# A new order within a tile of the scan, the carry in a spare column of h, a fifth product of w and B on GpSimd, and e minus g summed on TensorE

## The reference

```python
u, z = split(in_proj(seq)); u = silu(conv(u))
dt, Bm, Cm = split(x_proj(u))
dt = softplus(dt_proj(dt) + bias)
def step(h, ...):                        # h: 128 channels x 16 states
    h = exp(dt_t * A) * h + (dt_t * u_t) * B_t
    y = sum over states of h * C_t
y = (ys + u * D) * silu(z);  x = x + out_proj(y)
```

## Time and profile before

| | us |
|---|---|
| median of 3 runs | 1975.07 (1973.82 to 1977.28) |
| the profiled execution | 1973.6 |
| its span | 1971.8 |
| busy: PE, PE weight loads | 1445.4, 980.9 |
| busy: DVE, ACT, POOL | 1359.6, 928.1, 1138.6 |

### The profile page before, as it was taken

How to read it: one execution, slowest core, us unless ns; L and a number is a source line. 1 busy time by engine, 2 the same in 40 slices (tenths; PEclk the granted TensorE clock), 3 DMA queues, 4 the chain that set the end, 5 groups by cost and what they waited for, 6 DMA issues and landing times. The chain is left out here.

```text
span 1971.8 us, 28551 instructions
## 1 busy us (share of the span) xinstructions
PE 1445.4 (73%) x7776; PEld 980.9 (50%) x7777; DVE 1359.6 (69%) x1913; ACT 928.1 (47%) x1695; POOL 1138.6 (58%) x788
## 2 busy tenths in 40 slices
PE   6666766667656599999956766666667662799993
PEld 4333333333314499999834333333333222799992
DVE  2899999999995422222143999999999967444443
ACT  6666677667743011111136666677666731011111
POOL 0687788888880244444302888888878850355540
PEclk9889898998968699999968788998998866899996
DMA  3655566555638110111034565566555634111114
GB/s 110 147 135 121 129 144 146 125 126 134 145 79 354 54 41 32 38 37 36 26 126 98 129 138 121 129 143 139 134 121 135 148 136 188 38 48 48 47 41 152
DMA packets 75964, 217.61 MB, mean 110 GB/s; under 512 B 11856, under 2 KB 27408, under 8 KB 72592
## 3 DMA queue, kind: packets, MB, share of 16 engines
q1 hardware_dynamic: 67664, 194.53, 38.9%
q0 software_dynamic: 8256, 22.56, 3.5%
HBM read 178.34 MB, written 38.70 MB: 110 GB/s over the span
## 5 line engine op out<-in xcount | busy, mean ns | idle before, releaser
L669 POOL TENSOR_TENSOR L_hc<-L_h,L_cbq 128x1536 f32<-128x1536 f32 x192 | 660.1, 3438 | 210.6 <-DVE L_h L587 207.5
L492 ACT ACTIVATE ps<-L_dwq,L_negA 128x384 f32<-128x384 f32 x768 | 426.7, 574 | 227.4 <-DVE L_h L587 215.5
L364 PE MATMUL ps<-L_hc,same 128*32 128x384 f32 x1536 | 190.0, 571 | 238.9 <-POOL L_hc L669 238.9
L574 DVE TENSOR_TENSOR L_dbu<-L_dwq,ps 128x768 f32<-128x768 f32 x288 | 270.7, 941 | 29.4 <-DVE L_carry L649 13.1
L587 DVE TENSOR_TENSOR_SCAN L_h<-ps,L_h,L_dbu 128x384 f32<-128x384 f32 x288 | 275.0, 1002 | 12.9 <-ACT ps L492 12.8
L587 DVE TENSOR_TENSOR_SCAN L_h<-ps,L_carry,L_dbu 128x384 f32<-128x384 f32 x288 | 274.2, 1001 | 6.5 <-DVE L_dbu L574 4.7
L364 PEld LDWEIGHTS ps<-L_hc,same 128*32 128x32 f32 x1536 | 31.5, 113 | 358.2 <-POOL L_hc L669 324.3
L1151 DVE COPY Xn<-L_w 128x2048 f32 x86 | 107.6, 1253 | 117.1 <-PE ps L1101 108.3
L1134 ACT ACTIVATE L0e_hT<-ps 128x512 f32<-128x512 f32 x86 | 51.3, 597 | 267.2 <-PE ps L1101 267.2
L678 POOL TENSOR_TENSOR L_dbp<-L_dwq,L_cbq 128x768 f32<-128x768 f32 x96 | 175.1, 1824 | 0.0
L323 PE MATMUL ps<-Xn,L_fold 128*128 (+1 forms) x480 | 103.3, 368 | 89.2 <-DVE L_dw L595 89.2
(11 more groups left out here) (278 smaller groups left out, 2301.4 us busy)
## 6 DMA issues: line engine op xcount, KB each, us to landing
L_dwq<-dw_rows SPq DMA_DIRECT2D x192, 384.0 KB, 6.2
L_cbq<-cb_rows SPq DMA_DIRECT2D x192, 240.0 KB, 9.9
dw_rows<-L_dw SPq DMA_DIRECT2D x48, 384.0 KB, 2.3
L_w<-in_up SPq DMA_DIRECT2D x16, 1024.0 KB, 11.7
L_w<-in_down SPq DMA_DIRECT2D x8, 1024.0 KB, 26.6
tok_rows<-Xn SPq DMA_DIRECT2D x6, 768.0 KB, 13.1
L0s_got<-results SPq DMA_DIRECT2D x18, 256.0 KB, 2.9
L1s_got<-results SPq DMA_DIRECT2D x18, 256.0 KB, 3.5
```

The source lines that it names most:

```text
L364: mm = nc.tensor.matmul(y_ps[g * QW:(g + 1) * QW, :], same[:, 0:QW], hc[:, (k % 2) * Q + g, :], start=False, stop=(k == Q - 1))
L492: nc.scalar.activation(da(r, c), dwq[:, r, c % Q, 0, :], ACT.Exp, scale=negA[:, 0, c:c + 1]).then_inc(sem["da"], 1)
L574: nc.vector.tensor_tensor(dbu[:, at:at + 2, :], dwq[:, r, 2 * i:2 * i + 2, 1, :], spread(b_ps(r, k)), ALU.mult).then_inc(sem["dbu"], 1)
L669: nc.gpsimd.tensor_tensor(hc[:, at:at + Q, :], h[:, Q * k:Q * k + Q, :], cbq[:, r, k, :].unsqueeze(1).to_broadcast([P, Q, T]), ALU.mult).t ...
```

## The change

Five edits, all in the state-space block:

1. DVE's products of a tile go from six to five (`dbu` gets ten slots, no ring); POOL makes columns 10 and 11 too, in a new product at the head of its tile, from a sixth row of spread B (`QR` from 5 to 6).
2. `h` gets a spare column element (T + 1) that keeps the state from which each image starts; a scan reads its start from `h` itself, and the copy to `carry` and the wait for it go.
3. `lost` goes from POOL; TensorE adds e and, by a matrix of -1 on the diagonal (`minus`), subtracts g: four matmuls where three stood.
4. DVE: `times_u` stands after the tile's first scan (before: after the fourth), `gate` after the fourth (before: after the sixth). ACT: the block with the table loads stands after column 6 (before 7).
5. PE: within a tile, `spread_b` for k = 2 goes first, `u_in` is cut in two around the sum of y of the tile before, `z_in` follows, and the projections of tile t+2 come ahead of `sum_y(t, r, 0)`.

The core of the diff:

```diff
-QR = Q + 1
+QR = Q + 2
+SILU_AT = 6
...
-        carry = sb("carry", [P, 2, N])
+        carry = sb("carry", [P, N])
-        dbu = sb("dbu", [P, 6, T])
-        dbp = sb("dbp", [P, Q, T])
-        h = sb("h", [P, N, T])
+        dbu = sb("dbu", [P, 10, T])
+        dbp = sb("dbp", [P, 6, T])
+        h = sb("h", [P, N, T + 1])
...
             def add_log(t):
                 pe.wait_ge(sem["l"], t + 1)
                 nc.tensor.matmul(ua_ps, ident[:], sp["l"][:], start=False, stop=False)
-                pe.wait_ge(sem["lost"], t + 1)
-                nc.tensor.matmul(ua_ps, ident[:], sp["a"][:], start=False, stop=True).then_inc(sem["dt"], 1)
+                pe.wait_ge(sem["g"], t + 1)
+                nc.tensor.matmul(ua_ps, ident[:], sp["e"][:], start=False, stop=False)
+                nc.tensor.matmul(ua_ps, minus[:], sp["g"][:], start=False, stop=True).then_inc(sem["dt"], 1)
...
+                spread_b(t, r, 2)
+                if more == 2:
+                    u_in(t + 2, img2, (0, 1))
+                if not first:
+                    sum_y(t - 1, 1 - r, Q - 1)
+                if more == 2:
+                    u_in(t + 2, img2, (2, 3, 4))
                 if more:
-                    add_relu(t + 1)
-                    add_log(t + 1)
                     pe.wait_ge(sem["bc_out"], t + 2)
                     wait(pe, sem["res"], t - 1)
                     z_in(t + 1, img1)
-                if not first:
-                    sum_y(t - 1, 1 - r, Q - 1)
-                if more == 2:
-                    u_in(t + 2, img2, range(5))
-                spread_b(t, r, 2)
                 skip(t, r)
-                sum_y(t, r, 0)
-                if more:
-                    spread_b(t + 1, 1 - r, 0)
                 if more == 2:
                     project_dt(t + 2, r)
                     pe.wait_ge(sem["zs"], t + 2)
                     project_bc(t + 2, r)
+                sum_y(t, r, 0)
+                if more:
+                    spread_b(t + 1, 1 - r, 0)
...
                 sum_y(t, r, 2)
+                if more == 2:
+                    add_relu(t + 2)
+                    add_log(t + 2)
...
-                    if c == 7 and more:
+                    if c == SILU_AT and more:
...
                     k, i = (j + 1) // 2, (j + 1) % 2
-                    if k < Q - 1:
+                    if 2 * k + i < 5:
                         times_b(t, r, p, k, i)
                     elif j == N // 2 - 1 and not last:
                         times_b(t + 1, 1 - r, p + r, 0, 0)
                     scan(t, 2 * j, slot)
+                    if j == 0 and not last:
+                        times_u(t + 1, 1 - r, [(s_dw_row[r], 16 * (p + 1))])
                     scan(t, 2 * j + 1, slot)
-                    if j == 1 and not last:
-                        times_u(t + 1, 1 - r, [(s_dw_row[r], 16 * (p + 1))])
                     if not (isinstance(t, int) and t == 0):
-                        if j == 2:
+                        if j == 1:
                             gate(t - 1, 1 - r)
...
-                if not last:
-                    dve.wait_ge(sem["scan"], (2 * p + 2) * N)
-                    nc.vector.tensor_copy(carry[:, 1, :], h[:, :, T - 1]).then_inc(sem["carry"], 1)
-                    dve.wait_ge(sem["carry"], p + 2)
...
             def tile(t, r, p, last):
+                times_b(t, r, p, 0)
                 for k in range(Q):
                     times_c(t, r, p, k)
                     if k < 2:
-                        times_b(t, r, p, k)
-                    if k == 2 and not last:
-                        lost(t + 2)
+                        times_b(t, r, p, k + 1)
```

More of the change, by code:

```diff
@@ L258, in mamba @@
         sem = {k: new(f"{L}_{k}") for k in
-               ("u_in z_in u zs bc dt_in bc_out abs relu e f g l lost dt dt_out w b dbu dbu_p da scan carry hc skip y yz out "
+               ("u_in z_in u zs bc dt_in bc_out abs relu e f g l dt dt_out w b dbu dbu_p da scan carry hc skip y yz out "
                 "res").split()}
@@ L567, in times_b @@
                     dve.wait_ge(s_dw[r], 64 * (p + 1))
[L568 to L573, removed]
+                at = 4 * k + 2 * i
+                wait(dve, sem["scan"], (t - 1) * N + at + 2)
                 nc.vector.tensor_tensor(dbu[:, at:at + 2, :], dwq[:, r, 2 * i:2 * i + 2, 1, :], spread(b_ps(r, k)),
@@ L577, in scan @@
             def scan(t, c, slot):
-                k, g = c // Q, c % Q
+                k = c // Q
                 dve.wait_ge(sem["da"], t * N + c + 1)
-                if k < Q - 1:
-                    dve.wait_ge(sem["dbu"], 6 * t + c // 2 + 1)
+                if c < 10:
+                    dve.wait_ge(sem["dbu"], 5 * t + c // 2 + 1)
                 else:
-                    dve.wait_ge(sem["dbu_p"], 2 * t + g // 2 + 1)
+                    dve.wait_ge(sem["dbu_p"], 3 * t + (c - 10) // 2 + 1)
                 wait(dve, sem["hc"], Q * (t - 1) + k + 1)
[L585 to L588, removed]
+                first = h[:, c, T - 1:T] if slot is None else h[:, c, T - slot:T - slot + 1] if isinstance(slot, int) \
+                    else h[:, c, bass.ds(T - slot, 1)]
+                nc.vector.tensor_tensor_scan(h[:, c, 0:T], da(t % 2 if isinstance(t, int) else int(slot is None), c),
+                                             dbu[:, c, :] if c < 10 else dbp[:, c - 10, :], first, ALU.mult, ALU.add
                                              ).then_inc(sem["scan"], 1)
@@ L612, in _ @@
             nc.vector.tensor_scalar(diagD[:], ident[:], par("D"), None, ALU.mult).then_inc(s_fold, 1)
+            nc.vector.tensor_scalar(minus[:], ident[:], -1.0, None, ALU.mult).then_inc(s_fold, 1)
             times_u(0, 0, ())
             dve.wait_ge(s_tok, 6)
-            nc.vector.tensor_tensor(carry[:, 1, :].rearrange("p (k g) -> p k g", k=Q),
+            nc.vector.tensor_tensor(carry[:].rearrange("p (k g) -> p k g", k=Q),
                                     m["ones"][:, 0:N].rearrange("p (k g) -> p k g", k=Q),
@@ L676, in times_b @@
                     pool.wait_ge(s_dw[r], 64 * (p + 1))
-                    wait(pool, sem["scan"], t * N)
-                nc.gpsimd.tensor_tensor(dbp[:, 2 * i:2 * i + 2, :], dwq[:, r, 2 * i:2 * i + 2, 1, :],
-                                        spread(cbq[:, r, Q, :]), ALU.mult).then_inc(sem["dbu_p"], 1)
-            lost(0)
-            lost(1)
+                wait(pool, sem["scan"], (t - 1) * N + 12 + 2 * i)
+                groups, row = (2, Q + 1) if i == 0 else (2 * i - 2, Q)
+                nc.gpsimd.tensor_tensor(dbp[:, 2 * i:2 * i + 2, :], dwq[:, r, groups:groups + 2, 1, :],
+                                        spread(cbq[:, r, row, :]), ALU.mult).then_inc(sem["dbu_p"], 1)
             q = {k: tok[:, 2 + i:3 + i] for i, k in enumerate("arefgl")}
@@ L1370, in pack @@
     state = g("x_proj_w")[4:].reshape(2, Q, Q, P)
-    put("bc", np.concatenate([state[1].transpose(1, 0, 2), state[0, Q - 1][:, None]], 1).reshape(Q * QR, P).T)
+    put("bc", np.concatenate([state[1].transpose(1, 0, 2), state[0, Q - 1][:, None], state[0, Q - 2][:, None]], 1).reshape(Q * QR, P).T)
     put("brep", np.repeat(state[0].reshape(N, P), QW, 0).T)
```

19 lines of the change are left out of this document (9 added, 10 removed).

## The result

The changed kernel takes 2046.21 us (median of 4 runs, 2043.46 to 2047.22), against 1976.14 us for the kernel before in the same series: a ratio of 1.0354 (95% interval 1.0336 to 1.0372). It is slower by 3.5%.

The account below looks back on a forecast made before the run. DVE set the old 22.37 us period; a wait cycle through four engines, 23.49 us plus 0.5 for the clock, would set 24.0. 44 intervals gave +72 us, less 3, plus 1.5 for the median: 2044 us, range 2008 to 2092.

Parts of the forecast that it names:

- DVE's list: DVE's own work per tile, forecast to fall from 21.41 to 20.56 us, below the old period of 22.37 us.
- the ring: Wait cycle hc2, softplus sum, take_dt, times_u, scans, back to hc2: forecast to set the period, 24.0 us (23.5 to 24.6); 82%.
- the clock's share: Extra time per tile from TensorE's lowered clock between hc2's end and take_dt: 0.5 us, bounds 0 and 0.84 + 0.3.
- hc2's end to take_dt, full clock: From the end of POOL's third hc product to ACT's take_dt: 3.13 us plus 0.64 for one more matmul, 3.77.
- take_dt to times_u: From the start of ACT's take_dt to the start of DVE's times_u, which it releases: 0.79 us.
- times_u to the end of scan 7 (with ACT's hold): DVE's new order from times_u through scan 7, 10.00 us, plus 0.3 us waiting for ACT's table-load block.
- end of scan 7 to hc2's end: POOL's two hc products and one dbp product after DVE's scan 7: 8.63 us.
- no element is left out: Reason given for excluding any gain in POOL's hc products from 385-element rows; cost taken as 0, at most 0.15 us each.
- -3 us for the ends of the layers: After each layer's last times_u DVE's shorter work counts, one or two products less in each layer: -3 us.
- Rival A: DVE's work sets the time: period 20.9 us, 1907 us in total, faster; chance 9%.
- Rival B: No change in time: the round trip is 22.4 us, 1.1 us shorter than any sum at full clock; chance 3%.
- Rival C: TensorE's clock falls on every softplus sum: round trip 26.8 us, +192 us, 2167 us in total; chance 6%.

Follow-up runs that it names:

- adds_first: The changed kernel with TensorE's softplus sum for tile t+2 moved ahead of the third sum of y; 1896.09 us, ratio 0.9616 to the kernel before.
- old_places: The changed kernel with times_u, the gate and ACT's table block back at their old places in the tile; 2033.42 us, ratio 1.0317 to the kernel before.
- The fillers: The changed kernel with ten unused TensorE matmuls ahead of the second sum of y and five ahead of the third; 1995.02 us, ratio 1.0115.
- before_u_early: The kernel before with times_u alone moved behind the tile's first scan; 2063.3 us, ratio 1.0461.

## Why the prediction was right

**The mechanism.** It forecast that the softplus sum behind the third sum of y, with times_u moved ahead of scan 1, closes a ring through four engines that is longer than DVE's list. The wait ahead of times_u is there in every tile, adds_first removes it and with it 150 us, and the product on DVE is free with the ring and costs 37 us without. That DVE's saving is wasted behind the ring is shown, too. Of the runs that change something on this ring, all but old_places moved the way that it says, and in old_places another ring closed.

**The size, 2044 against 2046.21, by errors that cancel.** That the two are 2 us apart is luck: at full clock the ring was forecast 0.77 us too long, 34 us over 44 tiles, and the clock's share about as much too small. By terms, against the tile at full clock in the rows above:

| term | forecast, us | measured, us |
|---|---|---|
| hc2's end to take_dt, full clock | 3.77 | 3.76 |
| take_dt to times_u | 0.79 | 0.61 |
| times_u to the end of scan 7 (with ACT's hold) | 10.30 | 10.22 |
| end of scan 7 to hc2's end | 8.63 | 8.13 |
| sum at full clock | 23.49 | 22.72 |
| for the clock | 0.5 | 1.1 |
| period | 24.0 | 23.86 |

Scan 7's end is taken as hc1's start less 0.08 us, as before. The term of POOL was 0.5 us too long, since the 385-element rows made each hc product 0.27 us shorter; I had excluded a gain there ("no element is left out"), and that exclusion was wrong. The step from take_dt to times_u was 0.18 us too long, since I had taken it from a scan that waits for a decay. The clock's term was too small by 0.6 us: I had argued that TensorE's longer idling ahead of the second sum of y would bring the clock's fall forward and have it back by hc2's end. Three tiles in four show it low there. The fillers took 1.09 us a tile out of this stretch in the first layer, nearly the whole of the measured mean of 4.92 less 3.76 = 1.16. The number could have been had from the kernel before: over 44 tiles its trace has a mean of 4.22 us from hc2's end to take_dt where a tile at full clock has 3.11, so its mix of clocks cost 1.1 us, more than the 0.84 that I read from ACT's waits and then lowered to 0.5.

Outside the ring two more errors partly cancelled. I had put -3 us for the ends of the layers. In the profiled runs the two scan stages, from first to last scan, grew by 32.6 and 32.4 us, 65 together where 44 x 1.63 - 3 = 69 were forecast. The other 7.4 us of the 72.4 lie ahead of the first scan of the first layer (3.0), and behind the scan stages (1.7 and 2.7). I had put nothing there but the 0.2 us of the new matrix, which took 0.22. No run asks for their cause; adds_first has the same start and begins its scans 2.7 us earlier, so at least the first of them is not the change's.

**Rival A** (DVE's list sets the time) fell for the changed kernel, but its price was near the truth for the kernel without the ring: 1907 us forecast, 1896 measured. **Rival B** fell. **Rival C** (low clock on every softplus sum) fell as a whole and held in part: three tiles in four are slowed there in the steady part, at granted clocks of 0.67 to 0.70 in the three tiles behind the one walked above, and no period comes to its 26.8 us; the longest is 25.8. In before_u_early the clock was low there in every tile.

**What I costed at nothing.** The moved z projection: no wait shows it in the changed kernel, where DVE waits between 150 and 500 us for take_dt and, 2.2 us, for the output projection; it costs 79 us once times_u is late (old_places). It was cheap only beside the other move. The load of 24 rows: POOL's head product waits for it in the first tile of each layer only.

## What to carry to other kernels

When a step is moved ahead in one queue, follow what it waits for back through the other queues, until an engine comes twice: the sum of that round trip is the least period, however short each engine's own list is. The block to move was in TensorE's queue, which was not the busy engine: the softplus sum waited for nothing of its own but stood behind a sum that waited for POOL. And an order written by hand for several engines changes as one: a step that is free beside another move can cost 4% without it.

## What the runs showed of the hardware

An hc product on POOL (128x1536, 32-bit) takes 3.17 us when it reads rows that lie 385 elements apart, and 3.44 us with rows 384 or 392 apart. Why is open.

The period of times_u fell into a pattern of four tiles, 22.72, 24.44, 24.25 and 24.20 us, in both layers; in the group of four that was looked at, the softplus sum ran at granted clock 1.00 in the short one and at 0.67 to 0.70 in the three others. Rows of 385 elements, with shorter products on POOL, made the kernel before 0.7% slower; matmuls that do nothing made the changed one 2.5% faster (granted clock 0.98 where it was 0.88).
